# Recommendation kernel on one Trainium2 core: K's and Q's products on two halves of TensorE's rows, with other first loads and other filler waits

## The reference

```python
# r_F: F (2048, 64, 128); W (64, 64, 128); K_w, Q_w (128, 128); all fp32
Kf  = jnp.einsum('bjd,ed->bje', F, K_w)
S   = jnp.einsum('bid,bjd->bij', F, Kf)
out = jnp.einsum('bij,ijd->bid', S, W)
out = out + jnp.einsum('bid,ed->bie', F, Q_w)
```

## Time and profile before

| | us |
|---|---|
| median of 3 runs (607.44 to 609.15) | 608.06 |
| the profiled execution, its own time | 608.0 |
| its span, first to last instruction | 606.2 |
| PE busy / PEld busy | 597.5 / 527.0 |
| DVE busy / ACT busy | 398.7 / 401.5 |

### The profile page before, as it was taken

One profiled execution on the slowest core, in us unless ns is written; L12 is line 12 of the kernel. 1 busy time (PEld: TensorE's weight loads), 2 busy tenths in 40 slices (PEclk: granted clock), 3 DMA queues, 4 the chain that ended last, 5 costly groups with the idle time before them and its releaser, 6 DMA issues.

```text
span 606.2 us, 17908 instructions
## 1 busy us (share of the span) xinstructions
PE 597.5 (99%) x7693; PEld 527.0 (87%) x7693; DVE 398.7 (66%) x412; ACT 401.5 (66%) x698; POOL 0.2 (0%) x4
## 2 busy tenths in 40 slices
PE   9999999999999999999999999999999999999995
PEld 7888989889898898988889898898988989889894
DVE  6556757567685665947659475686756768567376
ACT  7978393874938659295692947839387493865830
POOL 0000000000000000000000000000000000000000
PEclk9999999999999999999999999999999999999998
DMA  8543847548575575755647566385755757457177
GB/s 324 239 141 145 322 169 282 199 177 312 189 281 173 212 262 208 280 200 208 246 183 284 204 248 241 140 322 173 285 197 186 304 196 282 173 211 259 66 279 278
DMA packets 29452, 137.60 MB, mean 227 GB/s; under 512 B 3264, under 2 KB 4032, under 8 KB 21312
## 3 DMA queue, kind: packets, MB, share of 16 engines
q1 hardware_dynamic: 20592, 75.38, 31.5%
q10 hardware_dynamic: 8784, 61.08, 28.4%
HBM read 69.34 MB, written 67.11 MB: 225 GB/s over the span
## 4 chain that ended last, share of the span: by engine, by line
PE 98%; DVE 1%; issue 1%; DVEq 0%
PE ps L501 20%; PE ps L440 20%; PE ps L442 19%; PE ps L441 19%; PE ps L527 18%; DVE o_sb L371 1%; PE ps L557 1%; DVEq L46 0%; PE ps L457 0%; PE ps L461 0%; PE ps L459 0%; DVE o_sb L380 0%; DVE f_hi L385 0%
## 5 line engine op out<-in xcount | busy, mean ns | idle before, releaser
L336 DVE TENSOR_TENSOR f_lo<-f_ring,f_hi 128x1024 fp32r<-128x1024 f32 x124 | 151.8, 1224 | 169.6 <-ACT f_hi L214 167.9
L228 ACT ACTIVATE q_out<-ps 128x512 f32<-128x512 f32 x256 | 156.9, 613 | 6.4
L219 ACT ACTIVATE kf<-ps 128x512 f32<-128x512 f32 x256 | 155.9, 609 | 3.4
L371 DVE TENSOR_TENSOR o_sb<-ps,q_out 128x1024 f32<-128x1024 f32 x127 | 145.1, 1213 | 19.3 <-PE ps L527 19.3
L237 ACT ACTIVATE s_t<-ps 128x512 f32<-128x512 f32 x32 | 19.1, 598 | 176.5 <-PE ps L501 176.5
L501 PE MATMUL ps<-f_ring,kf 128*64 128x64 f32 x4096 | 124.1, 222 | 0.4 <-issue 0.4
L501 PEld LDWEIGHTS ps<-f_ring,kf 128*64 128x64 f32 x4096 | 121.6, 138 | 2.9 <-issue 0.8
L527 PEld LDWEIGHTS ps<-s_t,w_sb 64*128 64x128 f32 x2048 | 115.6, 188 | 5.6 <-issue 5.6
L527 PE MATMUL ps<-s_t,w_sb 64*128 64x128 f32 x2048 | 118.6, 274 | 0.0
L440 PE MATMUL ps<-f_hi,k_hi 128*128 128x512 f32 x254 | 100.7, 397 | 0.0
L440 PE MATMUL ps<-f_hi,q_hi 128*128 128x512 f32 x256 | 99.9, 390 | 0.0
(11 more groups left out here) (36 smaller groups left out, 164.3 us busy)
## 6 DMA issues: line engine op xcount, KB each, us to landing
out<-o_sb SPq DMA_DIRECT2D x127, 512.0 KB, 3.5
f_ring<-f_t ACTq DMA_DIRECT2D x58, 1024.0 KB, 4.8
f_ring<-f_t SPq DMA_DIRECT2D x4, 1024.0 KB, 10.4
w_sb<-w SPq DMA_DIRECT2D x1, 2048.0 KB, 18.8
f_ring<-f SPq DMA_DIRECT2D x6, 256.0 KB, 5.1
out<-o_sb SPq DMA_DIRECT2D x2, 256.0 KB, 2.4
f_ring<-f SPq DMA_DIRECT2D x3, 128.0 KB, 2.6
f_ring<-f ACTq DMA_DIRECT2D x1, 128.0 KB, 4.3
```

Of the source, the lines that this page charges most:

```text
L219: nc.scalar.activation(kf[:, c // 2, c % 2 * CK:(c % 2 + 1) * CK, :, :].rearrange("d k h i -> d (k h i)"), ps[:, 2 * c % 8, :], COPY).then ...
L228: nc.scalar.activation(q_out[:, t % 2, :, :].rearrange("d i (h b) -> d i h b", h=2)[:, :, :, at:at + CK], q_bank(t * CHUNKS + c).rearrange ...
L336: nc.vector.tensor_tensor(f_lo[:, v % SPLIT, :], f_unit(v), f_hi[:, v % SPLIT, :].bitcast(F32), ALU.subtract).then_inc(flo_done, 1)
L371: nc.vector.tensor_tensor(o_sb[:, n % OBUF, :, :], ps[:, bank:bank + 2, :], q_out[:, t % 2, :, :].rearrange("d (s m) b -> d s (m b)", s=2) ...
```

## The change

The table of fillers is larger, and starts at the second tile and behind the fourth chunk of a tile. From the second tile on, each product is cut in two: over the lower 64 rows and over the upper 64 rows, three passes each into the same bank. `first_halves(n)` issues, in turn, Q's lower and K's upper passes of chunk n. `second_halves(n-1)` follows with K's lower and Q's upper passes of the chunk before. So a product is complete one step later, and a slot of the split parts is free one step later; ACT and DVE now wait for both `k_done` and `q_done` before they refill it. The first tile keeps the 128-row products.

The first loads are four: one array holds K_w, F's first chunk, Q_w and F's second chunk side by side. They land in the output buffers. F's first two chunks are loaded a second time into the ring (the first scores read them there). In the last tile the two last K products are made side by side, and the two last Q products too. The output buffer has another order of its columns; the last tile's rows use other banks, and its first block is summed in two parts by columns.

```diff
-FILL = {2: 58}
-FILL.update((t, 108) for t in range(3, TILES - 1))
-FILL[TILES - 1] = 132
+EARLY = 3
+FILL = {1: 395, 2: 374}
+FILL.update((t, 220 + t % 2) for t in range(3, TILES - 1))
+FILL[TILES - 1] = 300
...
+        raw = o_sb[:, 0:2, :, :, :].rearrange("d o x s b -> d (o x s b)")
+        k_raw, q_raw = raw[:, 0:D], raw[:, FC:FC + D]
+        f_raw = [raw[:, D:FC], raw[:, FC + D:2 * FC]]
...
-            load_half(0)
-            load_half(1)
-            load_half(3)
+            sp.dma_start(raw[:, 0:CUT], first[:, 0:CUT]).then_inc(first_in[0], 16)
+            sp.dma_start(raw[:, FC + CUT:2 * FC], first[:, FC + CUT:2 * FC]).then_inc(first_in[3], 16)
             for c in range(2, PIECES):
                 load_first(c)
+            load_first(0)
+            load_first(1)
             for p in range(2, RING):
                 load_f(p)
...
-            act.dma_start(k_raw, k_t).then_inc(k_in, 16)
-            act.dma_start(q_raw, q_t).then_inc(q_in, 16)
-            act.dma_start(f_half_cols(2), f_0[1, :, half_cols(0)]).then_inc(f_half[2], 16)
-            act.wait_ge(k_in, 16)
+            act.dma_start(raw[:, CUT:FC], first[:, CUT:FC]).then_inc(first_in[1], 16)
+            act.dma_start(raw[:, FC:FC + CUT], first[:, FC:FC + CUT]).then_inc(first_in[2], 16)
+            act.wait_ge(first_in[0], 16)
             nc.scalar.activation(k_hi[:, :], k_raw, COPY).then_inc(khi_done, 1)
-            split_half(0)
-            split_half(1)
-            act.wait_ge(q_in, 16)
+            act.wait_ge(first_in[1], 16)
+            nc.scalar.activation(f_hi[:, 0, half_cols(1)], f_raw[0][:, half_cols(1)], COPY).then_inc(fhi_first, 1)
+            act.wait_ge(first_in[2], 16)
             nc.scalar.activation(q_hi[:, :], q_raw, COPY).then_inc(qhi_done, 1)
-            split_half(2)
-            split_half(3)
+            act.wait_ge(first_in[3], 16)
+            nc.scalar.activation(f_hi[:, 0, piece_cols(1)], f_raw[1], COPY).then_inc(fhi_first, 1)
...
+                wait(dve, k_done, 2 * (c // 2 - SPLIT) + 2)
                 if c == 4:
                     dve.wait_ge(k_done, 1)
                 nc.vector.tensor_copy(f_hi[:, c // 2 % SPLIT, piece_cols(c)], f_cols(c)).then_inc(fhi_dve, 1)
-                dve.wait_ge(fhi_dve, c // 2)
+                dve.wait_ge(fhi_dve, c // 2 + 1)
...
+                    o_sb[:, n % OBUF, :, :, :].rearrange("d x s b -> d s x b"),
+                    ps[:, bank:bank + 2, :].rearrange("d s (x b) -> d s x b", x=IR),
+                    q_out[:, t % 2, :, :].rearrange("d (s m) b -> d s m b", s=2)[:, :, k * IR:(k + 1) * IR, :],
                     ALU.add).then_inc(out_done, 1)
...
+            dve.wait_ge(first_in[0], 16)
+            nc.vector.tensor_copy(f_hi[:, 0, half_cols(0)], f_raw[0][:, half_cols(0)]).then_inc(fhi_dve, 1)
+            dve.wait_ge(fhi_dve, 1)
+            low_half(0)
             dve.wait_ge(khi_done, 1)
             nc.vector.tensor_tensor(k_lo[:, :], k_raw, k_hi[:, :].bitcast(F32),
                                     ALU.subtract).then_inc(klo_done, 1)
-            low_half(0)
+            dve.wait_ge(fhi_first, 1)
             low_half(1)
             dve.wait_ge(qhi_done, 1)
             nc.vector.tensor_tensor(q_lo[:, :], q_raw, q_hi[:, :].bitcast(F32),
                                     ALU.subtract).then_inc(qlo_done, 1)
-            low_half(2)
-            low_half(3)
+            low_first(1)
...
+            def products(step):
+                n = min(step, TILES * CHUNKS - LATE)
+                if step < TILES * CHUNKS - LATE:
+                    return (q_of(n), q_done), (k_of(n), k_done)
+                if step == n:
+                    return (k_of(n), k_done), (k_of(n + 1), k_done)
+                return (q_of(n), q_done), (q_of(n + 1), q_done)
+            def k_of(c):
+                return ps[:, 2 * c % 8, :], k_hi, k_lo, c
+            def q_of(c):
+                return q_bank(c), q_hi, q_lo, c
+            def passes(dst, w_hi, w_lo, c, rows, first):
+                hi = f_hi[rows, c // 2 % SPLIT, piece_cols(c)]
+                lo = f_lo[rows, c // 2 % SPLIT, piece_cols(c)]
+                yield nc.tensor.matmul(dst, w_hi[rows, :], hi, start=first, stop=False)
+                yield nc.tensor.matmul(dst, w_hi[rows, :], lo, start=False, stop=False)
+                yield nc.tensor.matmul(dst, w_lo[rows, :], hi, start=False, stop=not first)
+            def first_halves(step):
+                (a, _), (b, _) = products(step)
+                for ins_a, ins_b in zip(passes(*a, lower, True), passes(*b, upper, True)):
+                    pass
+                ins_a.then_inc(half_done, 1)
+                ins_b.then_inc(half_done, 1)
+            def second_halves(step):
+                pe.wait_ge(half_done, 2 * (step - CHUNKS + 1))
+                (a, a_sem), (b, b_sem) = products(step)
+                for ins_b, ins_a in zip(passes(*b, lower, False), passes(*a, upper, False)):
+                    pass
+                ins_b.then_inc(b_sem, 1)
+                ins_a.then_inc(a_sem, 1)
...
+                    if t == 0:
+                        k_product(n)
+                        if c >= 4:
+                            pe.wait_ge(q_copied, n - 3)
+                        q_product(n)
+                        continue
+                    if c >= 4 and n < TILES * CHUNKS - LATE:
                         pe.wait_ge(q_copied, n - 3)
-                    if t < TILES - 1 or c < CHUNKS - LATE:
-                        q_product(n)
-                    for x in range(FILL.get(t, 0) * c // CHUNKS, FILL.get(t, 0) * (c + 1) // CHUNKS):
+                    first_halves(n)
+                    if c >= 1:
+                        second_halves(n - 1)
+                    a, b = max(c - EARLY, 0), CHUNKS - EARLY
+                    for x in range(FILL[t] * a // b, FILL[t] * max(c + 1 - EARLY, 0) // b):
                         pe.wait_ge(zeros_done, 1)
+                if t >= 1:
+                    second_halves(min((t + 1) * CHUNKS - 1, TILES * CHUNKS - LATE))
...
                if t == TILES - 1:
...
-                    for c in range(CHUNKS - LATE, CHUNKS):
-                        q_product(t * CHUNKS + c)
+                    first_halves(TILES * CHUNKS - LATE + 1)
+                    second_halves(TILES * CHUNKS - LATE + 1)
```

More of the change, by code:

```diff
@@ L80, in build @@
         ps = psum("ps", [P, 8, BANK])
-        f_half = [sem(f"f_half{n}") for n in range(4)]
+        first_in = [sem(f"first_in{n}") for n in range(4)]
         f_first = [sem(f"f_first{n}") for n in range(PIECES)]
         f_in = [sem(f"f_in{n}") for n in range(RING)]
-        k_in, q_in, w_in = sem("k_in"), sem("q_in"), sem("w_in")
+        w_in = sem("w_in")
         o_stored = [sem(f"o_stored{n}") for n in range(OBUF)]
@@ L349, in both_f @@
                 dve.wait_ge(q_done, 2 * (v - SPLIT) + 2)
+                dve.wait_ge(k_done, 2 * (v - SPLIT) + 2)
                 nc.vector.tensor_copy(f_hi[:, v % SPLIT, :], f_unit(v)).then_inc(fhi_dve, 1)
-                dve.wait_ge(fhi_dve, 3 + sum(1 for x in BOTH if x <= v))
+                dve.wait_ge(fhi_dve, 4 + sum(1 for x in BOTH if x <= v))
                 low_unit(v)
@@ L450, in q_product, with k_halves @@
                       f_lo[:, c // 2 % SPLIT, piece_cols(c)]).then_inc(q_done, 1)
-            def k_halves(c):
-                for h in range(2 * c, 2 * c + 2):
-                    dst, cols = ps[:, 2 * c, half_cols(h % 2)], half_cols(h)
-                    pe.wait_ge(fhi_first, h + 1)
+            def k_halves():
+                pe.wait_ge(khi_done, 1)
+                for h in range(2):
+                    dst, cols = ps[:, 0, half_cols(h)], half_cols(h)
+                    pe.wait_ge(fhi_first if h else fhi_dve, 1)
                     nc.tensor.matmul(dst, k_hi[:, :], f_hi[:, 0, cols], start=True, stop=False)
+                    pe.wait_ge(flo_first, h + 1)
+                    nc.tensor.matmul(dst, k_hi[:, :], f_lo[:, 0, cols], start=False, stop=False)
                     pe.wait_ge(klo_done, 1)
-                    nc.tensor.matmul(dst, k_lo[:, :], f_hi[:, 0, cols], start=False, stop=False)
-                    pe.wait_ge(flo_first, h + 1)
-                    ins = nc.tensor.matmul(dst, k_hi[:, :], f_lo[:, 0, cols], start=False, stop=True)
+                    ins = nc.tensor.matmul(dst, k_lo[:, :], f_hi[:, 0, cols], start=False, stop=True)
                 ins.then_inc(k_done, 1)
@@ L511, in scores_tile @@
                             pe.wait_ge(q_copied, 13 + e // 2)
+                        if e == 0:
+                            for c in range(2):
+                                pe.wait_ge(f_first[c], 16)
                     elif e % 2 == 0:
@@ L518, in row_block @@
             def row_block(t, k):
-                bank = 2 * k % 8
+                bank = row_bank(t, k)
+                split = t == TILES - 1 and k == 0
                 for x in range(IR):
                     m = k * IR + x
```

(8 more changed lines are left out.)

88 lines of the change are left out of this document (44 added, 44 removed).

## The result

The changed kernel takes 617.59 us (median of 5 runs, 616.97 to 617.99), the kernel before 608.06 beside it (607.31 to 609.15): ratio 1.0153, 95% interval 1.0140 to 1.0167. It is 9.5 us slower. The forecast was 5.3 us faster, and the range ended at 613.5: sign and range are both wrong.

What follows compares the result with a forecast made beforehand. TensorE, busy 597.5 of 606.2 us, was taken to bound the kernel. The terms -0.6 + 4.1 + 2.7 - 10.6 - 0.8 - 0.1 gave -5.3 us, so 602.7 us, with an 8-in-10 range of 596.5 to 613.5.

Steps and rivals of the forecast that it cites:

- The pair's gap: Middle product stages: pairs of half-row matmuls 218.3 ns apart instead of 227; 10.6 us less over products(3) to (14).
- Rival 1: Product stages: the 14 ns between matmuls belong to fp32r and stay with pairs; 613.4 us, chance 0.22.
- The fillers: Wait instructions 0.107 us apart starve TensorE in products(1), +4.1 us, and products(2), +2.7; hidden in products(3) to (14).
- products(15): The last tile's product stage: its 90 pairs, not its fillers, decide; 19.8 us against 20.6, so 0.8 less.
- The two last Q products as pairs: End of the last tile: together with the earlier first half sum, 0.1 us less.
- rival 5: Sequencer gets nearly twice as many matmuls ahead, so products(1) and (2) starve less; 599.4 us, chance 0.04.
- The borders: Scores: instruction fetches fall elsewhere, as some stages take 7.84 us and not 7.62; up to 1.5 us either way.
- The start: First tile: the third chunk's product begins earlier thanks to the new load order; 0.6 us less.
- rival 2: Product stages: ACT's copies and DVE's low parts come too late and stall TensorE; 606 to 614 us, chance 0.07.
- rival 3: Fillers stay hidden in products(1) and (2), since the sequencer takes ready waits faster when starved; 593.9 us, chance 0.08.
- rival 4: Middle product stages: a pair's gap is about half of rows', saving 0.24 us more each; 599.6 us, chance 0.07.
- rival 6: Product stages: the two halves of a pair don't run side by side; about 920 us, chance 0.02.

Runs made afterwards that it cites:

- e5: e4 with the first tile's chunks 8 to 15 multiplied as fp32, bf16, fp32r on the lower rows, fp32 on the lower rows; 626.71 us, one run.
- e9: e4 with the first tile's chunks 8 to 15 as fp32r with 64-column weights, bf16 pairs, fp32 pairs, 128-column fp32r; bf16 pairs stood 0.225 us apart.
- e2: The changed kernel with no filler waits at all; 611.17 us, ratio 1.0055.
- e1: The changed kernel without filler waits in products(1) and products(2); 614.12 us, ratio 1.0104.
- e4: The changed kernel with 128-row products instead of pairs and the fillers of the kernel before; 612.67 us, ratio 1.0077.
- e8: e4 with 90 fillers in products(3) to (15), in place of 108 and, in the last, 132; 607.16 us, ratio 0.9988.
- e7: The changed kernel with fillers cut to 128 in products(1), 180 in products(2) and 220 in products(15); 612.24 us, ratio 1.0072.
- e10: e1 with each output store cut to a quarter of its bytes; 602.53 us, ratio 0.9908.

## Why the prediction was wrong

**The pair's gap: the step that failed.** "I take the gap of the nearest rows, which have the same tile of 64 rows by 128 columns in the same alternation: 213.3 + 5 = 218.3 ns." It measured 226.7. The rows stage shares its tile with the pairs, but is fp32 and takes two cycles a column, and that is what the small gap goes with (e5, e9). Rival 1 had the pair right for a nearly right reason: fp32r keeps its 14 ns, though bf16 has 12 too. Its own time, 613.4 us, is still 4.2 too low, for the fillers and the borders below. The term was -10.6 us; measured is -1.11 in products(3) to (14). Even that is not the gap but the switch at the stage's end, which my sum took out without a word (a stage takes 22.00 us with it, 0.11 + 96 x 0.227 = 21.90 without). Rows saved 1.14, by a switch at their start that was not in the sum at all. Rival 1 should have been the forecast: an fp32r neighbour of 256 columns with the same gap was in the same trace, closer in what it streams than rows are.

**The fillers: mechanism right, size low.** +4.1 and +2.7 forecast, +5.65 and +4.00 measured. The waits do stand 0.106 us apart and starve TensorE. Lines L559, wait instructions in products(1), after (count, ns, first and last start):

```profile
L559 PEldq EVENT_SEMAPHORE  x179: 51/51/51, 37.8 to 61.3; - x179
```

They begin 3.1 us into the stage, where I had 2.84. But a step of 16 waits takes about 1.80 us, not 1.71: the twelve matmuls and their weight loads take their own 0.1 us of the sequencer, and over some thirteen steps this is 1.2 of the missing 1.5. In the last tile too: products(15) was to save 0.8 and lost 0.4. Its fillers cost 0.5 (21.03 us against 20.53 in e2), with steps of up to 1.5 us where six pairs of 226.7 ns need 1.36. The two last Q products as pairs, part of the -0.1 in the sum, lost 0.25 (1.85 us against 1.60).

The Trainium skill (TensorE: Matmul & The Clock Gate, Architectural detail, under Engine queue depths) says that TensorE's queue holds 64. At 37.8 us of the changed kernel 14 matmuls had been handed over and not begun, with their weight loads 28; near the end of a stage of the kernel before it was 17 matmuls, with loads 34. No run here shows 64, and rival 5 with it is out.

**The borders: the unknown with bounds too narrow.** I gave the moved instruction fetches "up to 1.5 us either way". In the changed kernel itself they cost 1.7 us, just over, but in its variants up to 8.0 - 1.6 = 6.4 us against before (e1). What I had taken for small scatter of scores stages, 7.84 and not 7.62, had a cause that the queue's packets and a count of instructions would have shown.

The Trainium skill (Runtime: NRT & Kernel Launch, Instruction fetch mechanics) says that blocks of 256 instructions are streamed in and that crossing a border is mostly hidden. The trace agrees with the block. It is not hidden where 256 instructions last 3.73 us and the DMA engines are full.

**What was right.** The start (-0.6 forecast, -0.46 measured). ACT and DVE were not late: the longest wait of a product's matmul for a low part is 0.4 us, once in the run, so rival 2 is out. Rivals 3, 4, 5 and 6 are out by the stages above. The sum with measured sizes is -0.46 + 9.65 - 1.11 + 0.63 - 1.14 + 1.70 + 0.31 = +9.6 us.

## What to carry to other kernels

Before giving a matmul the gap of another, compare what it streams per cycle, not only the shape of its tile; here a contraction of full width cut into row halves gained nothing in its streaming, only 0.2 us a tile at the switches into rows. Waits that only take room in the list cost the sequencer 0.106 us each and are free only while matmuls are queued ahead. And where a stage of short instructions coincides with a full DMA queue, count TensorE's instructions to the next multiple of 256, and read in the trace when each block's fetch is served: in this kernel, moving the borders was worth 5.5 us (e4 against e8). Then measure: e7 had the borders of scores in nearly the same place as e8 and was 5.1 us slower.

## What the runs showed of the hardware

- Satisfied wait instructions of TensorE stand 0.106 us apart, though each is 51 ns long.
- At full clock, matmuls with a weight load each stand at: fp32r of 512 columns 226.7 ns, bf16 225, fp32 429 a record (two records a matmul), fp32r of 128 columns about 111 (whole rows only). The other three are the same within 2 ns on 128 rows alone and in pairs of 64.
- TensorE's instructions come in blocks of 16,384 bytes, 256 instructions. With full stores, the fetch of the first border in scores(1) to (15) is served 0 to 2.4 us after the first matmul behind the border, that of the second up to 5.2 (e4). At borders in rows it is anything from 2.1 us before to 1.3 after. The transfer takes 0.9 to 2.0 us, and a TensorE that waits for it goes on 1.2 to 1.6 us after its end. e10 shows that the holes come from the output stores. Why a fetch waits 1 us at some borders and 2 or more at others, with all DMA engines full at both, was not tried.
